# Four layers on a graph: the second batch's attention changes from whole fp32 weights to fp16 high and low parts

## The chip, the cores and the metric

The kernel runs on one core of a Trainium2 chip. The metric is the device time of one execution in microseconds (us). Times inside an execution are counted from the first instruction of the profiled span.

## The reference, cut to what matters

There are 8 batches of 1024 nodes with 128 features (`x`), one dense 1024x1024 matrix `adj`, and four layers, each followed by a residual and a layer norm. Layer 1 is the attention that this change is about:

```python
Q = x @ q
K = x @ k
A = jnp.einsum('bnd,bmd->bnm', Q, K)
A = A / jnp.sqrt(jnp.float32(input_dimension))
A = jnp.tanh(A / 8.0) * 8.0
A = jnp.exp(A) * A_shape            # A_shape is adj
A = A / jnp.sum(A, axis=-1, keepdims=True)
out = A @ x @ v
...
x = _layernorm(x + _L0_gnn_ref(x, adj, ...))   # rows scaled to unit norm
x = _layernorm(x + _L1_gnn_ref(x, adj, ...))   # the attention
x = _layernorm(x + _L2_gnn_ref(x, adj, ...))
x = _layernorm(x + _L3_gnn_ref(x, adj, ...))
```

## The kernel before

All engines run one program each, written out in a fixed order, and meet only at semaphores. The names: PE is the matmul engine, DVE the vector engine, ACT the scalar engine, POOL computes the inverse roots of the norms, SP issues the transfers. Batches are numbered 0 to 7; "the second attention" is that of batch 1.

**Precision by parts.** Most matmuls take an fp32 value as two fp16 tensors, a high part (written by ACT as a copy) and a low part (written by DVE as value minus high part). A product is then three fp16 matmuls: high by high, high by low, low by high.

**One attention** has eight steps t = 0 to 7, one for each block of 128 keys:

- `scores(i, t)` on PE: 6 matmuls of 512 columns into one of two PSUM regions (`r0`, `r1`).
- `exponent(i, t)` on ACT: a Tanh (L414) and an Exp (L416) into slot t % 4 of the fp32 ring `att`.
- `mask(i, t)` on DVE (L907): `att` times `adjT`; it raises the semaphore `pm`.
- For attentions with i >= FULL, `p_hi_part` on ACT (L292, `ph`) and `p_lo_part` on DVE (L912, `pl`) split the slot into the fp16 rings `p_hi` and `p_lo`.
- `attend(i, t)` on PE adds the step to the sums in PSUM `av`. With i < FULL it waits for `pm` and issues 8 fp32 matmuls of 129 columns, with `att` as the stationary and `v_full` as the moving side (L1473). With i >= FULL it waits for `pl` and issues 24 fp16 matmuls (L1482, L1484, L1485) from `p_hi`, `p_lo` and the parts of V (`vhi`, `vlo`, `vhs`).

FULL is 2 before: batches 0 and 1 use whole fp32 weights, batches 2 to 7 use parts. The whole V of batch 1 is written into the memory of `p_lo`, which is free until batch 2; that is why the trace names the fp32 operand of the second attention `p_lo`. A slot of `att` may be overwritten once `attend` has read it (whole weights), or once `p_lo_part` has read it (parts).

**Around the second attention** (PE's `start()`, L1533 on): PE starts with `scores(1, 0)`, finishes `attend(0, 6)` and `attend(0, 7)`, and then alternates `scores(1, t)`, `attend(1, t)` and `adj_x2_part(0, k)` (6 matmuls of 512 columns each, the third layer's product of batch 0). After `adj_x2_part(0, 3)` comes `sum_x2` (L1398), which DVE waits for in `sums_read` (L795). After `adj_x2_part(0, 7)` comes `back(1)`: two parts of `adj_x0`, and then `project` with `w2s` (L1314), which waits for DVE's `y2_lo(0, 1)` (L788), which in turn waits for ACT's `y2_hi(0, 1)`, a copy of what `adj_x2_part(0, 4)` to `(0, 7)` summed.
DVE's own order in this stretch is: masks, and between them the end of batch 0's attention (`row_sums`, residual), its layer norm (`ln_begin` L584 on, root on POOL, `ln_shift` L618, `ln_norm`), `x2_lo`, `sj_step`, `weights_split`, and after the last mask `sums_read`, `sums`, `y2_lo(0, 0)`, `sj_step`, `x0_lo(2)`, `l2_read`, `l2_rank_one`, `y2_lo(0, 1)`. ACT's `copy_x2` writes the high part that `x2_lo` needs.

Of the kernel before, what the change touches and what calls it, by code (L numbers as in the profile page):

```python
# [40 lines left out]
L2_LINKS = 4  # L41
V_CHUNKS = 5
AVW = 130
FULL = 2
RING = 4
AHEAD = 3

# [30 lines left out]
def adj_resnorm(nc, x, adj, adj_t, w_first, w2, w3, rows, out):  # L78
    ctx = ExitStack()
    with ctx:  # L80
# [62 lines left out]
        minus_half = sb("minus_half", [P, C])  # L143
        small = sb("small", [P, 5, 8, C])
        rsum, rinv = sb("rsum", [P, 9]), sb("rinv", [P, C])
        v_full = [t[:].rearrange("p r n -> p (r n)").bitcast(F32)[:, 0:C * AVW].rearrange("p (c d) -> p c d", c=C) for t in (p_hi, p_lo)]
        junk = att[:].rearrange("p r n -> p (r n)").bitcast(F16)
        last_junk = u[:].rearrange("p c d -> p (c d)").bitcast(F16)[:, 0:N]
        row_bufs = [t[:].rearrange("p c d -> p (c d)") for t in (pq, u, tmp)]
# [140 lines left out]
        def _(act):  # L290
# [54 lines left out]
            def copy_x2(b):  # L345
                act.wait_ge(S["ln1_v"], b + 1)
                act.wait_ge(S["ln1_a"], b + 1)
                if not is_first(b, 0):
                    act.wait_ge(S["y2_mm"], 2 * b)
                copy(x2s[:, 0], xas[b % 2][:], X_UP).then_inc(S["x2_hi"], 1)  # L350
# [46 lines left out]
            def v_whole(b, src):  # L397
                for h in range(2):
                    act.wait_ge(S["v_mm"], 2 * b + h + 1)
                    copy(v_full[b][:, half_chunks(h), 0:D], cd(src[:])[:, half_chunks(h)], W_DOWN / LO_UP).then_inc(S["v_hi"], 1)  # L400
# [5 lines left out]
            def exponent(i, t):  # L406
                t8, s = i * C, t % RING
                act.wait_ge(S["s_mm"], t8 + t + 1)
                if RING <= t8 + t < FULL * C + RING:
                    act.wait_ge(S["av_mm"], t8 + t - RING + 1)  # L410
                elif t8 + t >= RING:
                    act.wait_ge(S["pl"], t8 + t - RING + 1 - FULL * C)
                dst = (r1, r0)[(t + (i == 0)) % 2]
                nc.scalar.activation(att[:, s], dst[:], ACT.Tanh, scale=c_tanh).then_inc(S["th"], 1)  # L414
                act.wait_ge(S["th"], t8 + t + 1)
                nc.scalar.activation(att[:, s], att[:, s], ACT.Exp, scale=TANH_CAP).then_inc(S["ex"], 1)  # L416
# [14 lines left out]
            def start():  # L431

                scale_adj(0, 3)
                y0_hi(0, 0, r1[:, half(0)])
                y0_hi(0, 1, r1[:, half(1)])
                degrees(0, 3)
                x0_hi(1)
                for h in range(2):
                    act.wait_ge(S["dg_mm"], h + 1)
                    copy(d_hi[:, half(h)], r0[:, half(h)], 1.0 / ADJ_UP).then_inc(S["dg_hi"], 1)  # L440
                scale_adj(3, C)
                degrees(3, 6)
                act.wait_ge(S["p0_mm"], 2)
                y0_hi(1, 0, m7[:])
                norm(0, 0, xas[0], V_CHUNKS)
                x1t_hi(0, r1)
                degrees(6, 7)
                g_hi(0, r2)
                y0_hi(1, 1, av[:, 2])
                v_whole(0, r1)  # L450
                for t in range(C):
                    exponent(0, t)
                    if t == 5:
                        degrees(7, 8)
                    if t == 6:
                        norm(0, 1, xas[1], V_CHUNKS)
                x1t_hi(1, r0)
                g_hi(1, r1)
                v_whole(1, r0)
                for t in range(C):  # L460
                    exponent(1, t)
                    if t == 3:
                        norm(1, 0, xas[0], V_CHUNKS)
                        copy_x2(0)
                act.wait_ge(S["p0_mm"], 4)
                y2_hi(0, 0)
                x0_hi(2)
# [106 lines left out]
        def _(dve):  # L574
# [304 lines left out]
            def sj_low():  # L879
                return tt(one_sj[:, :, 2], sj[:], one_sj[:, :, 1], ALU.subtract)  # L880
# [96 lines left out]
            def start():  # L977
# [54 lines left out]
                        ln_norm(0, 1, xas[1])  # L1032
                x1t_lo(1, r0)
                g_lo(1, r1)
                row_scales()
                x0_max(2)
                mask(1, 0)
# [2 lines left out]
                    l_ = attention_residual(0, j)  # L1040
                l_.then_inc(S["e1a"], 1)
                mask(1, 1)
                dve.wait_ge(S["e1a"], 1)
                ln_begin(1, 0, xas[0])
                mask(1, 2)
                x0_scale_read(2)
                x0_scales(2)
                ln_shift(1, 0)
                ln_norm(1, 0, xas[0])
                mask(1, 3)  # L1050
                x2_lo(0)
                mask(1, 4)
                sj_ch = Count(dve, S["sj_c"], 0, 5)
                for k_ in range(2):
                    sj_step(sj_ch, 0, k_)
                mask(1, 5)
                weights_split(3, 4)
                w_ch.end()
                mask(1, 6)
                sj_low().then_inc(S["sj_l"], 1)  # L1060
                mask(1, 7)
                l2_ch = Count(dve, S["l2_c"], 0, L2_LINKS)
                sums_read(0, r0)
                sums(0)
                y2_lo(0, 0)
                sj_step(sj_ch, 0, 2, False)
                sj_step(sj_ch, 0, 3)
# [223 lines left out]
        def _(pe):  # L1291
# [197 lines left out]
            def start():  # L1489
# [38 lines left out]
                scores(1, 0)  # L1528
                attend(0, 6)
                attend(0, 7)  # L1530
                pe.wait_ge(S["v_hi"], 4)
                scores(1, 1)
                next_scores(1, 2)  # L1533
                next_scores(1, 3)
# [229 lines left out]
```

## Time and profile before

| what | value |
|---|---|
| median of 3 runs | 659.71 us (659.68 to 660.11) |
| the profiled execution, its own time | 661.49 us |
| its span, first to last instruction | 659.0 us |
| PE busy | 631.6 us, 96% |
| DVE busy | 568.4 us, 86% |
| ACT busy | 400.5 us, 61% |
| mean granted clock of PE | 0.995 |

The profiled execution took 661.49 us, of which 2.49 us lie outside the span. Busy time of PE counts matmuls from their start to a modelled end, and they overlap, so the start-to-start times of its groups are the better measure of what a group costs. Idle time that a view puts in brackets is the time in which an engine stood waiting, with the instruction that ended it.

### The profile page before, as it was taken

What the parts mean: (1) busy time and instruction counts of PE and PEld (TensorE: products, weight loads), DVE (VectorE), ACT (ScalarE), POOL (GpSimd) and SP (SyncE); (2) the same over time, 40 slices, a digit from 0 to 9 for tenths busy, and PEclk for the clock granted to TensorE, in tenths of its full rate; (3) what the DMA queues carried; (4) which work ended last, traced back from release to release, by engine and by line L of the source; (5) the groups of instructions that cost most, each with busy time, mean ns of one, the idle gap of its engine ahead of it and who ended that gap; (6) DMA issues with size and microseconds to landing.
All of it is one profiled execution on the core that took longest, in us unless ns stands there. A gap on an engine that the chain in (4) does not pass through costs nothing.

```text
span 659.0 us, 17533 instructions
## 1 busy us (share of the span) xinstructions
PE 631.6 (96%) x7446; PEld 489.0 (74%) x7446; DVE 568.4 (86%) x1514; ACT 400.5 (61%) x706; POOL 73.4 (11%) x50
## 2 busy tenths in 40 slices
PE   8899899999999999999999999999999999889994
PEld 3457667698677976799667986789667986549894
DVE  6889687889899899889899899889898898989635
ACT  5879583354955669265873659365892649432522
POOL 0101210010002200210002200031002100020002
PEclk9999999999999999999999999999999999999998
DMA  8710000000000200002000200002000000000012
GB/s 334 260 65 1 1 1 1 0 31 6 2 1 2 66 1 2 1 2 66 2 1 1 66 2 1 2 3 66 1 1 2 8 29 1 1 1 2 2 34 65
DMA packets 12589, 18.74 MB, mean 28 GB/s; under 512 B 608, under 2 KB 9056, under 8 KB 12512
## 3 DMA queue, kind: packets, MB, share of 16 engines
q1 hardware_dynamic: 12512, 17.63, 8.1%
q8 instruction: 58, 0.95, 0.6%
q14 instruction: 19, 0.16, 0.1%
HBM read 13.44 MB, written 4.19 MB: 27 GB/s over the span
## 4 chain that ended last, share of the span: by engine, by line
PE 60%; DVE 22%; ACT 10%; issue 4%; POOL 2%; DMA 1%; SPq 0%; ACTq 0%; DVEq 0%; POOLq 0%
PE r L1314 13%; PE r L1316 13%; PE r L1315 13%; ACT att L414 5%; DVE p_lo L912 4%; DVE att L907 4%; PE r L1362 4%; DVE stats L584 2%; POOL small L249 2%; ACT p_hi L292 2%; DVE x L816 2%; PE av L1473 2%; PE r L1320 2%; PE av L1314 2%; PE av L1316 2%
## 5 line engine op out<-in xcount | busy, mean ns | idle before, releaser
L249 POOL TENSOR_TENSOR small<-small,minus_half 128x8 f32<-128x8 f32 (+1 forms) x40 | 69.0, 1729 | 573.7 <-DVE small L611 309.9
L907 DVE TENSOR_TENSOR att<-att,adjT 128x1024 f32<-128x1024 f32 x64 | 78.1, 1222 | 11.9 <-ACT att L416 11.8
L414 ACT ACTIVATE att<-r,coef 128x1024 f32<-128x1024 f32 x64 | 70.5, 1101 | 20.3 <-PE r L1316 19.7
L1314 PE MATMUL r<-xq,a_hi 128*128 128x128 f16 x448 | 76.0, 219 | 0.0
L1315 PE MATMUL r<-xq,a_hi 128*128 128x128 f16 x448 | 76.0, 219 | 0.0
L1316 PE MATMUL r<-xq,a_lo 128*128 128x128 f16 x448 | 76.0, 219 | 0.0
L1314 PE MATMUL r<-rs,a_hi 128*128 128x128 f16 x448 | 75.9, 219 | 0.0
L1315 PE MATMUL r<-rs,a_hi 128*128 128x128 f16 x448 | 75.8, 219 | 0.0
L1316 PE MATMUL r<-rs,a_lo 128*128 128x128 f16 x448 | 75.8, 219 | 0.0
L416 ACT ACTIVATE att<-att 128x1024 f32<-128x1024 f32 x64 | 67.7, 1057 | 2.0
L912 DVE SCALAR_TENSOR_TENSOR p_lo<-p_hi,att 128x1024 f16<-128x1024 f16 x48 | 58.6, 1222 | 0.0
L292 ACT ACTIVATE yT<-r 128x512 f16<-128x512 f32 x18 | 10.6, 595 | 69.6 <-PE r L1316 69.4
L292 ACT ACTIVATE p_hi<-att 128x1024 f16<-128x1024 f32 x48 | 50.1, 1043 | 2.4 <-DVE att L907 2.4
L1315 PEld LDWEIGHTS r<-xq,a_hi 128*128 128x128 f16 x448 | 43.8, 98 | 0.1
L1314 PEld LDWEIGHTS r<-rs,a_hi 128*128 128x128 f16 x448 | 43.8, 98 | 0.0
L1315 PEld LDWEIGHTS r<-rs,a_hi 128*128 128x128 f16 x448 | 43.8, 98 | 0.0
L1314 PEld LDWEIGHTS r<-xq,a_hi 128*128 128x128 f16 x448 | 43.8, 98 | 0.0
L1316 PEld LDWEIGHTS r<-xq,a_lo 128*128 128x128 f16 x448 | 43.8, 98 | 0.0
L1316 PEld LDWEIGHTS r<-rs,a_lo 128*128 128x128 f16 x448 | 43.8, 98 | 0.0
L340 ACT ACTIVATE outb<-outb,small 128x128 f32<-128x128 f32 x56 | 22.8, 481 | 24.2 <-DVE small L618 24.2
L1482 PE MATMUL av<-vhib,p_hi 128*128 128x129 f16 x192 | 33.6, 220 | 3.0 <-DVE p_lo L912 2.9
L1314 PE MATMUL m<-a_hi,x2s 128*128 128x512 f16 x96 | 36.4, 379 | 0.0
(424 smaller groups left out, 2114.9 us busy)
## 6 DMA issues: line engine op xcount, KB each, us to landing
adjT<-in_adj_t SPq DMA_DIRECT2D x8, 512.0 KB, 8.5
out<-outb SPq DMA_DIRECT2D x7, 512.0 KB, 3.4
x<-in_x SPq DMA_DIRECT2D x6, 512.0 KB, 4.8
pq<-in_adj SPq DMA_DIRECT2D x2, 512.0 KB, 8.8
u<-in_adj SPq DMA_DIRECT2D x2, 512.0 KB, 9.3
tmp<-in_adj SPq DMA_DIRECT2D x2, 512.0 KB, 9.8
x2s<-in_adj SPq DMA_DIRECT2D x2, 512.0 KB, 9.6
x<-in_x SPq DMA_DIRECT2D x2, 256.0 KB, 2.7
```

Source lines behind the costliest of these rows:

```text
L249: return nc.gpsimd.tensor_tensor(dst, src, minus_half[:, 0:src.shape[-1]], ALU.pow)
L292: return nc.scalar.activation(dst, src, ACT.Copy, scale=scale, **more)
L340: l_ = nc.scalar.activation(t[:, j], t[:, j], ACT.Identity, scale=small[:, k_, ROOT, j:j + 1], bias=small[:, k_, SHIFT, j:j + 1])
L414: nc.scalar.activation(att[:, s], dst[:], ACT.Tanh, scale=c_tanh).then_inc(S["th"], 1)
L416: nc.scalar.activation(att[:, s], att[:, s], ACT.Exp, scale=TANH_CAP).then_inc(S["ex"], 1)
L907: tt(att[:, s], att[:, s], adjT[:, t, :], ALU.mult).then_inc(S["pm"], 1)
L912: stt(p_lo[:, s], p_hi[:, s], -LO_UP, att[:, s], ALU.mult, ALU.add).then_inc(S["pl"], 1)
L1314: mm(dst, s_hi, m_hi, start=start, stop=False, skip_group_check=True)
L1315: mm(dst, s_hi, m_lo, start=False, stop=False, skip_group_check=True)
L1316: return mm(dst, s_lo, m_hi, start=False, stop=stop, skip_group_check=True)
L1362: l_ = mm(dst[:, a:e], x0s[:, x_part, m], src, start=(n_ == 0 and x_part == 0 and hi is a_hi and a == base), stop=False, skip_group_check= ...
L1482: mm(acc, p_hi[:, s, chunk(j)], vhi[:, t, 0:D + 1], start=(t == 0 and j % 3 == 0), stop=False, skip_group_check=True)
```

## The change

FULL goes from 2 to 1. Batch 0 keeps whole fp32 weights; batch 1 now takes parts, as batches 2 to 7 do. On ACT, V of batch 1 is written as a high part (`v_hi`) in place of whole (`v_whole`), a scaled copy of it (`v_scaled`, 128x1024) is added, and eight `p_hi_part` stand each after the next step's `exponent`. On DVE, `v_lo` (two instructions of 128x512) and eight `p_lo_part` are added. On PE each of eight `attend` steps has 24 fp16 matmuls in place of 8 fp32 ones and waits for `pl` in place of `pm`, and `scores(1, 1)` waits for `v_lo`, since it overwrites the PSUM region that holds V. One small memset of V's constant column at the very start goes. No other instruction changes its place in the order.

```diff
--- before.py
+++ after.py
@@ -41,7 +41,7 @@
 L2_LINKS = 4
 V_CHUNKS = 5
 AVW = 130
-FULL = 2
+FULL = 1
 RING = 4
 AHEAD = 3
 
@@ -143,7 +143,7 @@
         minus_half = sb("minus_half", [P, C])
         small = sb("small", [P, 5, 8, C])
         rsum, rinv = sb("rsum", [P, 9]), sb("rinv", [P, C])
-        v_full = [t[:].rearrange("p r n -> p (r n)").bitcast(F32)[:, 0:C * AVW].rearrange("p (c d) -> p c d", c=C) for t in (p_hi, p_lo)]
+        v_full = [t[:].rearrange("p r n -> p (r n)").bitcast(F32)[:, 0:C * AVW].rearrange("p (c d) -> p c d", c=C) for t in (p_hi,)]
         junk = att[:].rearrange("p r n -> p (r n)").bitcast(F16)
         last_junk = u[:].rearrange("p c d -> p (c d)").bitcast(F16)[:, 0:N]
         row_bufs = [t[:].rearrange("p c d -> p (c d)") for t in (pq, u, tmp)]
@@ -456,12 +456,17 @@
                         norm(0, 1, xas[1], V_CHUNKS)
                 x1t_hi(1, r0)
                 g_hi(1, r1)
-                v_whole(1, r0)
+                v_hi(1, r0)
                 for t in range(C):
                     exponent(1, t)
+                    if t == 0:
+                        v_scaled(1)
+                    if t >= 1:
+                        p_hi_part(1, t - 1)
                     if t == 3:
                         norm(1, 0, xas[0], V_CHUNKS)
                         copy_x2(0)
+                p_hi_part(1, C - 1)
                 act.wait_ge(S["p0_mm"], 4)
                 y2_hi(0, 0)
                 x0_hi(2)
@@ -1032,6 +1037,7 @@
                         ln_norm(0, 1, xas[1])
                 x1t_lo(1, r0)
                 g_lo(1, r1)
+                v_lo(1, r0)
                 row_scales()
                 x0_max(2)
                 mask(1, 0)
@@ -1040,28 +1046,36 @@
                     l_ = attention_residual(0, j)
                 l_.then_inc(S["e1a"], 1)
                 mask(1, 1)
+                p_lo_part(1, 0)
                 dve.wait_ge(S["e1a"], 1)
                 ln_begin(1, 0, xas[0])
                 mask(1, 2)
+                p_lo_part(1, 1)
                 x0_scale_read(2)
                 x0_scales(2)
                 ln_shift(1, 0)
                 ln_norm(1, 0, xas[0])
                 mask(1, 3)
+                p_lo_part(1, 2)
                 x2_lo(0)
                 mask(1, 4)
+                p_lo_part(1, 3)
                 sj_ch = Count(dve, S["sj_c"], 0, 5)
                 for k_ in range(2):
                     sj_step(sj_ch, 0, k_)
                 mask(1, 5)
+                p_lo_part(1, 4)
                 weights_split(3, 4)
                 w_ch.end()
                 mask(1, 6)
+                p_lo_part(1, 5)
                 sj_low().then_inc(S["sj_l"], 1)
                 mask(1, 7)
+                p_lo_part(1, 6)
                 l2_ch = Count(dve, S["l2_c"], 0, L2_LINKS)
                 sums_read(0, r0)
                 sums(0)
+                p_lo_part(1, 7)
                 y2_lo(0, 0)
                 sj_step(sj_ch, 0, 2, False)
                 sj_step(sj_ch, 0, 3)
@@ -1528,7 +1542,7 @@
                 scores(1, 0)
                 attend(0, 6)
                 attend(0, 7)
-                pe.wait_ge(S["v_hi"], 4)
+                pe.wait_ge(S["v_lo"], 2)
                 scores(1, 1)
                 next_scores(1, 2)
                 next_scores(1, 3)
```

The functions that it newly calls for batch 1, as they stand for the later batches:

```python
def v_scaled(b):
    act.wait_ge(S["v_hi"], 2 * (b + 1))
    copy(vhss[b % 2][:, :, 0:D], vhis[b % 2][:, :, 0:D], 1.0 / LO_UP).then_inc(S["v_s"], 1)
def v_lo(b, src):
    for h in range(2):
        hc = half_chunks(h)
        split_lo(vlos[b % 2][:, hc], cd(src[:])[:, hc], W_DOWN, vhis[b % 2][:, hc, 0:D], "v", 2 * b + h + 1)
def p_lo_part(i, t):
    t8, s = i * C, t % RING
    dve.wait_ge(S["ph"], t8 + t + 1 - FULL * C)
    stt(p_lo[:, s], p_hi[:, s], -LO_UP, att[:, s], ALU.mult, ALU.add).then_inc(S["pl"], 1)
```

The next rows are from the order of instructions on DVE, from `mask(1, 1)` to the instruction behind `mask(1, 2)`. In the changed kernel all these lines stand 5 further down, so the mask is L912 and `p_lo_part` is L917. Before:

```order
L907 TENSOR_TENSOR att<-att,adjT 128x1024
L584 BN_STATS stats<-xa 128x6 x8
L599 TENSOR_TENSOR small<-stats 128x8
L600 SCALAR_TENSOR_TENSOR small<-stats 128x8
L601 SCALAR_TENSOR_TENSOR small<-stats 128x8
L608 SCALAR_TENSOR_TENSOR small<-small 128x8
L613 SCALAR_TENSOR_TENSOR small<-small 128x8
L907 TENSOR_TENSOR att<-att,adjT 128x1024
L662 TENSOR_SCALAR xpow<-m 128x1
```

The same place on DVE of the changed kernel:

```order
L912 TENSOR_TENSOR att<-att,adjT 128x1024
L917 SCALAR_TENSOR_TENSOR p_lo<-p_hi,att 128x1024
L589 BN_STATS stats<-xa 128x6 x8
L604 TENSOR_TENSOR small<-stats 128x8
L605 SCALAR_TENSOR_TENSOR small<-stats 128x8
L606 SCALAR_TENSOR_TENSOR small<-stats 128x8
L613 SCALAR_TENSOR_TENSOR small<-small 128x8
L618 SCALAR_TENSOR_TENSOR small<-small 128x8
L912 TENSOR_TENSOR att<-att,adjT 128x1024
L917 SCALAR_TENSOR_TENSOR p_lo<-p_hi,att 128x1024
L667 TENSOR_SCALAR xpow<-m 128x1
```

A `p_lo_part` now stands between each mask and the work that followed it, here ahead of the layer norm of batch 0.

The end of the same stretch on DVE before, from `mask(1, 6)` on: `sj_low`, `mask(1, 7)`, `sums_read` and `sums` (L795 to L805), then `y2_lo(0, 0)`.

```order
L907 TENSOR_TENSOR att<-att,adjT 128x1024
L880 TENSOR_TENSOR one_sj<-sj,one_sj 128x8
L907 TENSOR_TENSOR att<-att,adjT 128x1024
L795 COPY xs<-r 128x3
L802 TENSOR_SCALAR xb<-xs 128x128
L803 TENSOR_TENSOR xs<-xs 128x1
L805 TENSOR_SCALAR xb<-xs,wjp 128x128
L788 SCALAR_TENSOR_TENSOR yT<-m,yT 128x512
```

The same place on DVE of the changed kernel:

```order
L912 TENSOR_TENSOR att<-att,adjT 128x1024
L917 SCALAR_TENSOR_TENSOR p_lo<-p_hi,att 128x1024
L885 TENSOR_TENSOR one_sj<-sj,one_sj 128x8
L912 TENSOR_TENSOR att<-att,adjT 128x1024
L917 SCALAR_TENSOR_TENSOR p_lo<-p_hi,att 128x1024
L800 COPY xs<-r 128x3
L807 TENSOR_SCALAR xb<-xs 128x128
L808 TENSOR_TENSOR xs<-xs 128x1
L810 TENSOR_SCALAR xb<-xs,wjp 128x128
L917 SCALAR_TENSOR_TENSOR p_lo<-p_hi,att 128x1024
L793 SCALAR_TENSOR_TENSOR yT<-m,yT 128x512
```

Three more `p_lo_part` stand here; the last one is behind `sums` and ahead of `y2_lo(0, 0)`.

On ACT before, from the Tanh of `exponent(1, 3)` to the Exp of `exponent(1, 5)`, with the norm and `copy_x2` of batch 0 between:

```order
L414 ACTIVATE att<-r,coef 128x1024
L416 ACTIVATE att<-att 128x1024
L340 ACTIVATE xa<-xa,small 128x128 x3
L292 ACTIVATE x2s<-xa 128x1024
L414 ACTIVATE att<-r,coef 128x1024
L416 ACTIVATE att<-att 128x1024
L414 ACTIVATE att<-r,coef 128x1024
L416 ACTIVATE att<-att 128x1024
```

The same place on ACT of the changed kernel:

```order
L414 ACTIVATE att<-r,coef 128x1024
L416 ACTIVATE att<-att 128x1024
L292 ACTIVATE p_hi<-att 128x1024
L340 ACTIVATE xa<-xa,small 128x128 x3
L292 ACTIVATE x2s<-xa 128x1024
L414 ACTIVATE att<-r,coef 128x1024
L416 ACTIVATE att<-att 128x1024
L292 ACTIVATE p_hi<-att 128x1024
L414 ACTIVATE att<-r,coef 128x1024
L416 ACTIVATE att<-att 128x1024
```

One copy to `p_hi` stands behind each Exp, and it needs the mask of the step before.

## Rows read from the trace of the kernel before

**Rows 1.** The page: busy time by engine; the chain that ended last, by engine.

```profile
PE 631.6 (96%) x7446; PEld 489.0 (74%) x7446; DVE 568.4 (86%) x1514; ACT 400.5 (61%) x706; POOL 73.4 (11%) x50
...
PE 60%; DVE 22%; ACT 10%; issue 4%; POOL 2%; DMA 1%; SPq 0%; ACTq 0%; DVEq 0%; POOLq 0%
```

**Rows 2.** Busy time per engine in two stretches: second attention, third attention.

```profile
85.61:117.96 32.35, 31.06 (x223) 22.94 (x222) 25.50 (x59) 16.15 (x18) 2.55 (x1) 1.00 0.00 1
163.44:193.00 29.56, 29.51 (x269) 18.48 (x269) 26.34 (x40) 26.35 (x27) 0.00 (x0) 1.00 0.01 2
```

**Rows 3.** Tiles av, p_hi and p_lo by shape: duration min/median/max in ns, first and last start.

```profile
L1482 PE MATMUL av<-vhi,p_hi x192: 219/220/231, 170.9 to 498.6; 128*128 128x129 f16 x192
...
L1485 PE MATMUL av<-vhs,p_lo x192: 218/220/220, 171.0 to 498.7; 128*128 128x129 f16 x192
...
L1473 PE MATMUL av<-p_lo,att x128: 273/275/357, 85.7 to 116.6; 128*128 128x129 f32 x128
...
L292 ACT ACTIVATE p_hi<-att x48: 1037/1041/1059, 167.8 to 567.2; 128x1024 f16<-128x1024 f32 x48
...
L292 ACT ACTIVATE p_lo<-r x2: 599/599/599, 76.0 to 76.7; 128x512 f32<-128x512 f32 x2
...
L912 DVE SCALAR_TENSOR_TENSOR p_lo<-p_hi,att x48: 1216/1221/1230, 169.4 to 568.3; 128x1024 f16<-128x1024 f16 x48
```

**Rows 4.** Timeline of PE around second attention, and one third-attention step: start, length.

```profile
85.75 2.03 PE L1473 MATMUL av<-p_lo,att 128*128 128x129 f32 x16
87.62 0.38 PE L1314 MATMUL r<-gb_,x1Tb 128*128 128x512 f16 x1
...
88.91 1.95 PE L1473 MATMUL av<-p_lo,att 128*128 128x129 f32 x16
90.70 0.38 PE L1314 MATMUL r<-gb_,x1Tb 128*128 128x512 f16 x1
...
108.36 0.17 PE L1398 MATMUL r<-one_sj,x2s 128*128 128x3 f16 x1
...
119.54 0.23 PE L1314 MATMUL r<-w2s,yT 128*128 128x128 f16 x1
...
170.90 0.22 PE L1482 MATMUL av<-vhi,p_hi 128*128 128x129 f16 x1
...
172.26 0.38 PE L1314 MATMUL r<-g,x1T 128*128 128x512 f16 x1
```

**Rows 5.** Timeline of DVE; a bracket is idle time before, and its releaser.

```profile
80.50 1.23 DVE L907 TENSOR_TENSOR att<-att,adjT 128x1024 f32<-128x1024 f32 x1 [2.27 <-ACT att L416]
...
85.37 1.23 DVE L907 TENSOR_TENSOR att<-att,adjT 128x1024 f32<-128x1024 f32 x1 [0.76 <-ACT att L416]
86.51 1.64 DVE L584 BATCH_NORM_STATS2 stats<-xa 128x6 f32<-128x128 f32 x8
...
91.50 0.17 DVE L618 SCALAR_TENSOR_TENSOR small<-small 128x8 f32<-128x8 f32 x1 [0.82 <-POOL small L249]
...
96.29 1.23 DVE L907 TENSOR_TENSOR att<-att,adjT 128x1024 f32<-128x1024 f32 x1 [0.86 <-ACT att L416]
...
104.13 1.22 DVE L907 TENSOR_TENSOR att<-att,adjT 128x1024 f32<-128x1024 f32 x1
108.94 0.16 DVE L795 COPY xs<-r 128x3 f32<-128x3 f32 x1 [3.59 <-PE r L1399]
...
118.79 0.69 DVE L788 SCALAR_TENSOR_TENSOR yT<-r,yT 128x512 f16<-128x512 f32 x1 [1.84 <-ACT yT L292]
```

**Rows 6.** Timeline of ACT, second attention; and the root on POOL in the chain.

```profile
84.28 1.06 ACT L416 ACTIVATE att<-att 128x1024 f32<-128x1024 f32 x1
...
101.11 1.11 ACT L414 ACTIVATE att<-r,coef 128x1024 f32<-128x1024 f32 x1 [0.66 <-PE r L1316]
...
88.92 2.56 POOL small L249
```

**Rows 7.** Busy time and granted clock (the 1.00 and 0.77) in two thin stretches.

```profile
65.00:70.00 5.00, 3.20 (x24) 2.40 (x21) 3.40 (x13) 2.10 (x5) 4.20 (x2) 1.00 0.00 2
650.00:655.00 5.00, 0.44 (x8) 0.26 (x5) 4.75 (x27) 0.93 (x3) 2.02 (x2) 0.77 0.36 105
```


## The prediction

> **What bounds the kernel now.** I read the page first: PE is busy for 96% of the span, DVE for 86%, ACT for 61%, and the chain that ended last runs 60% on PE and 22% on DVE [rows 1]. So any microsecond that PE stands still in the middle is likely to reach the end, and DVE is the engine that is close enough to make it stand still. The change touches one stage, so I read that stage alone. In the 32.35 us from the first `attend` of batch 1 to the end of its last product, PE is busy 31.06, DVE 25.50 and ACT 16.15 us [rows 2]: PE sets the pace, DVE has 6.85 us of idle time, ACT 16.2. The third attention, which already uses parts, shows what the form needs: PE 29.51 of 29.56 us with DVE at 26.34 and ACT at 26.35 [rows 2]. There PE never starves, but that stage carries less other DVE work between its masks than this one.
>
> **What the change gives on PE.** A fp32 step starts at 88.91 and what follows it starts at 90.70: 1.79 us for 8 matmuls. A step with parts starts at 170.90 and its follower at 172.26: 1.36 us for 24 [rows 4]. The single durations (275 ns for fp32, 220 ns for fp16 [rows 3]) overlap, so only starts count. The change saves 0.43 us per step, 8 x 0.43 = 3.4 us in all, if PE never waits.
>
> At this place a rule of the Trainium skill speaks against the change. The rows give 1.36 / 24 = 57 ns per pair of weight load and matmul [rows 4]. The page "TensorE: Matmul & The Clock Gate", section "Back-to-back issue gap", puts the sustained pace of such pairs at about 81 ns with 128 columns. By it a step would be an estimated 24 x 81 ns = 1.94 us, longer than the fp32 step, and PE would lose 1.2 us over the eight instead of gaining 3.4. The sum goes by the rows; the other pace is a rival below.
>
> **What it costs on ACT.** Eight copies to `p_hi` at 1.04 us each [rows 3] are 8.3 us, and `v_scaled` is a copy of the same 128x1024 size, about 1.0 us. Writing V's high part instead of whole V is two copies of the same shape at 0.6 us [rows 3], no change. ACT has 16.2 us idle in the stage [rows 2]; its Tanh and Exp move 1 us later per step but stay ahead of the masks that wait behind DVE's own work. Price: nothing. If that cover were gone, ACT would still have only 9.3 us to place in 16.2.
>
> **What it costs on DVE.** `v_lo` is two instructions of 128x512, like the two of `g_lo`, under 1.3 us for both (half of a `p_lo_part` each [rows 3], with their fixed part). They stand in the 2.27 us in which DVE waits before the mask at 80.50 [rows 5], so they cost nothing, and PE's new wait for them (about 78.5) is over when it comes to `scores(1, 1)` behind two fp32 steps (after 81). Eight `p_lo_part` last 1.221 us each [rows 3], as a mask does. Two instructions of this size start 1.14 us apart (85.37 and 86.51 [rows 5]), so they add 8 x 1.14 = 9.12 us. That is more than the 6.85 us that DVE has free [rows 2]. Where it comes out is found by walking through DVE's order; each row is a starting time before, and behind it I put the shift. The price of the order change is in this walk.
>
> 1. `mask(1, 1)` stays at 85.37. `p_hi_part(1, 0)` follows the Exp at 84.28 [rows 6], so it ends about 86.4, and the first `p_lo_part` starts at 86.5 and ends at 87.7. PE's first `attend` started at 85.75 [rows 4], and now starts at about 87.8: a first hole of 2 us, while the layer norm of batch 0 begins at 86.51 + 1.14.
> 2. Ahead of `ln_shift` at 91.50 DVE stood 0.82 us for POOL's root (2.56 us from 88.92 [rows 6]). Two `p_lo_part` stand before it now. DVE is free at 90.68 + 2.28 = 92.96, the root is there at 91.50 + 1.14 = 92.64. Shift: +1.46.
> 3. `mask(1, 4)` at 96.29 had waited 0.86 us for its Exp [rows 5]. That Exp stands behind `copy_x2`, so it shifts by 1.46 to 97.75; DVE is free at 95.43 + 1.46 + 1.14 = 98.03. Shift: +1.74.
> 4. `mask(1, 7)` at 104.13 has three more ahead of it: +1.74 + 3.42 = +5.16, it starts at 109.29. The sixth `p_lo_part`, for t = 5, ended just before, at about 109.30. After the mask and the seventh DVE is free at 109.29 + 2.28 = 111.57.
> 5. `sums_read` at 108.94 waited 3.59 us for `sum_x2` [rows 5]. PE's `attend(1, 5)` now waits for that sixth `p_lo_part`: 109.35, plus 1.36, plus 1.29 for `adj_x2_part(0, 3)` (six matmuls of 512 columns, as 87.62 to 88.91 [rows 4]), plus 0.58 from the start of `sum_x2` to DVE (108.36 to 108.94 [rows 4, 5]): 112.58. Shift: +3.64, and DVE still waits 1.0 us here.
> 6. The eighth `p_lo_part` follows: +4.78. `y2_lo(0, 1)` at 118.79 had 1.84 us idle ahead [rows 5]: DVE reaches it at 116.95 + 4.78 = 121.73, +2.94. PE's side would allow +3.64 - 2 x 0.43 = +2.78. The later one counts: **+2.9 us**.
>
> As a balance: 9.12 added, less 0.82, 0.86 and 1.84 us of holes filled and 2.6 of the 3.59, gives 3.0. PE's `project` at 119.54 [rows 4] moves by this, to 122.5, and the 3.4 us saved on PE lie inside its new holes (2 us each ahead of `attend` 0, 1 and 2, less later).
>
> **What is late next.** In the third attention PE is busy 29.51 of 29.56 us [rows 2] at the same clock, so there is no hole to give the delay back, and `back(1)` is in order behind `project` on all engines. Each transfer of a later batch is released by these same engines. The shift reaches the end whole. Batches 2 to 7 are unchanged.
>
> **The sum.** The profiled execution took 661.49 us (span 659.0); with +2.9 it would take 664.4. It lies 1.78 us above the median of the runs, 659.71; the same shift on the median gives **662.6 us**, slower by 0.44%. Own bounds: at 1.22 us a piece (the full duration, no overlap of starts) the eight cost 0.6 us more, +3.5. If the wait in step 5 did not come about (`attend(1, 5)` had its weights a little earlier), up to 1.0 us goes, +1.9. So this case spans 661.5 to 663.3.
>
> **The rivals.**
> - *DVE hides its new work and PE's saving counts (faster).* PE ahead by up to 3.4 us: 656.3. For it speaks ACT's and DVE's idle time in the stage and the full PE of the third attention [rows 2]. Against it: 9.12 us don't fit into 6.85. It decides at a `p_lo_part` of about 0.8 us or less, (9.12 - 2.9) / 8; the rows show 1.22 in every form [rows 3]. Chance 0.06.
> - *The delay is given back (no change).* Should 2 of the 2.9 us be absorbed in `back(1)`, the time is 660.6. Chance 0.09.
> - *Parts run at a slower pace on PE than in the third attention.* Bounded by the fp32 step, 1.79 us from start to start [rows 4]: step 5 gives +3.64 + 0.43 = +4.07 and the last two steps give nothing back, so PE decides: +4.1 us, 663.8. Against it: 192 fp16 instructions of each form with a median of 220 ns [rows 3], and the 57 ns pace. Chance 0.06. The page named above would make such a step longer still, an estimated +4.5 us in all by the same steps; the trace does not agree with it.
> - *PE's clock falls in the new holes.* Three holes of 2 us each between 85.6 and 97 leave PE about half busy. Granted clock stayed at 1.00, 2.4 GHz, where it was busy 3.20 of 5 us, and fell (0.77 in the mean) only where it was busy 0.44 of 5 [rows 7]. At 1.2 GHz the next 6.6 us of matmuls take twice as long; part of that hides in the waits for DVE, so up to +6.6 on top, 666 to 669. Chance 0.05.
>
> **How the numbers follow.** My case has a chance of 0.74. A measurement of this kernel can tell about 0.2%, 1.3 us, from no change: 658.4 to 661.0. Slower: 0.74 + 0.06 + 0.05 = 0.85; same 0.09; faster 0.06. The range leaves out the faster case, the absorbed one and the fallen clock (0.20) and reaches from my lower bound to the slow pace, 661.5 to 663.8, with 0.3 to 0.4 us more on both sides, since each of the walk's three places where a bracket is subtracted from a start is good to about 0.1 us: 661.2 to 664.2.
>
> **What the profile after would show.** Right: PE's first `attend` of batch 1 at about 87.8; brackets of about 2 us on PE that end with `p_lo` L917, three of them; DVE without a bracket before `ln_shift` and `mask(1, 4)`, with about 1 us before `sums_read`; `project` at 122.4; every later row of PE later by the same 2.9. Wrong: DVE brackets as long as before (then ACT is the cause, and the copies were not free), `project` at 119 or earlier, or steps of `attend` that start more than 1.4 us ahead of their followers.

## The result, and the profile after

The change made the kernel slower: the ratio to the kernel before is 1.004, with a 95% interval from 1.0026 to 1.0053. It is a ratio of means over 12 executions each, 663.31 against 660.80 us, a difference of 2.5 us. The medians are 663.57 and 660.26 us, 3.3 us apart. The forecast was +2.9 us, 662.6 us, in a range from 661.2 to 664.2; it started from a median of 659.71 us over three executions, and on 660.26 us the same +2.9 gives 663.2 us. A few executions of several kernels, the kernel before among them, took over 100 us longer than the rest (773.6, 937.56 and 1677.14 us), and no ratio in this document counts them.

A part of each time lies outside the profiled span. In the changed kernel this is 2.0 to 2.2 us; in the kernel before it was 2.49 us in the profiled execution and 2.4 us in the mean of the 62 that were measured beside the experiments. Why it differs is not known. It makes a difference of times about 0.3 us smaller than what happens inside the span.

The page of the changed kernel, busy time by engine and the chain that ended last:

```profile
PE 628.9 (95%) x7510; PEld 484.7 (73%) x7510; DVE 578.4 (87%) x1523; ACT 409.0 (62%) x715; POOL 73.4 (11%) x50
...
PE 60%; DVE 24%; ACT 8%; issue 4%; POOL 2%; DMA 1%; SPq 0%; ACTq 0%; DVEq 0%; POOLq 0%
```

Against [rows 1], PE has 2.7 us less to do and DVE 10.0 us more; DVE's share of the chain rose from 22 to 24%. The span grew from 659.0 to 661.4 us.

Busy time per engine (PE, PEld, DVE, ACT, POOL), granted clock, DMA: the thin part of the second attention, the whole of it, and the third attention of the changed kernel:

```profile
85.61:97.00 11.39, 6.14 (x70) 4.16 (x69) 11.18 (x31) 10.44 (x13) 2.55 (x1) 1.00 0.00 0
85.61:121.00 35.39, 28.73 (x293) 18.98 (x292) 33.88 (x67) 24.23 (x27) 2.55 (x1) 1.00 0.00 1
...
166.00:195.60 29.60, 29.55 (x272) 18.56 (x270) 26.21 (x40) 26.51 (x27) 0.00 (x0) 1.00 0.01 1
```

In [rows 2] PE was the full engine of this stage and DVE had 6.85 us free. Now DVE is busy 33.88 of 35.39 us and PE only 28.73. In the first 11.39 us PE works barely more than half the time, and its granted clock is still 1.00. The third attention is as it was.

Timeline of PE of the changed kernel, from the first `scores` of batch 1 to `project`; a bracket is the hole ahead, with what ended it:

```profile
76.63 0.39 PE L1328 MATMUL r<-gb_,x1Tb 128*128 128x512 f16 x1
...
87.75 0.22 PE L1496 MATMUL av<-vhib,p_hi 128*128 128x129 f16 x1 [1.99 <-DVE p_lo L917]
...
89.10 0.38 PE L1328 MATMUL r<-gb_,x1Tb 128*128 128x512 f16 x1
...
92.18 0.23 PE L1496 MATMUL av<-vhib,p_hi 128*128 128x129 f16 x1 [1.62 <-DVE p_lo L917]
...
96.63 0.23 PE L1496 MATMUL av<-vhib,p_hi 128*128 128x129 f16 x1 [1.63 <-DVE p_lo L917]
...
104.90 0.23 PE L1496 MATMUL av<-vhib,p_hi 128*128 128x129 f16 x1 [0.20 <-DVE p_lo L917]
...
108.93 0.23 PE L1496 MATMUL av<-vhib,p_hi 128*128 128x129 f16 x1 [1.21 <-DVE p_lo L917]
...
121.97 0.23 PE L1328 MATMUL r<-w2s,yT 128*128 128x128 f16 x1
```

A step with parts is as short as forecast: 87.75 to 89.10 is 1.35 us against 1.79 [rows 4]. Five of the eight steps wait for a low part. A bracket counts from the modelled end of the matmul before, so start to start the holes are longer: `scores` from 89.10 would be done at 90.39 (1.29 us), and the next step starts at 92.18, a hole of 1.79 us where the bracket says 1.62. In this way the five are 7.5 us. The steps save 8 x 0.44 = 3.5 us, and a hole of 1.5 us for a Tanh is gone. Before, this line of PE's timeline had it (1.45 us from start to start):

```profile
95.23 0.39 PE L1314 MATMUL r<-gb_,x1Tb 128*128 128x512 f16 x1 [1.29 <-ACT att L414]
```

So the delay is 7.5 - 3.5 - 1.5 = 2.5 us.

Timeline of DVE of the changed kernel, at the places of [rows 5]:

```profile
80.37 1.23 DVE L912 TENSOR_TENSOR att<-att,adjT 128x1024 f32<-128x1024 f32 x1 [0.93 <-ACT att L416]
...
86.38 1.22 DVE L917 SCALAR_TENSOR_TENSOR p_lo<-p_hi,att 128x1024 f16<-128x1024 f16 x1
87.52 1.64 DVE L589 BATCH_NORM_STATS2 stats<-xa 128x6 f32<-128x128 f32 x8
...
92.74 0.16 DVE L623 SCALAR_TENSOR_TENSOR small<-small 128x8 f32<-128x8 f32 x1
...
97.63 1.22 DVE L912 TENSOR_TENSOR att<-att,adjT 128x1024 f32<-128x1024 f32 x1
...
108.86 1.22 DVE L912 TENSOR_TENSOR att<-att,adjT 128x1024 f32<-128x1024 f32 x1
...
112.17 0.16 DVE L800 COPY xs<-r 128x3 f32<-128x3 f32 x1 [0.95 <-PE r L1413]
...
121.23 0.68 DVE L793 SCALAR_TENSOR_TENSOR yT<-r,yT 128x512 f16<-128x512 f32 x1
```

The hole before the first mask shrank from 2.27 to 0.93 us and took `v_lo` in. The holes of 0.82, 0.86 and 1.84 us are gone, and that of 3.59 us is 0.95.

The start of the kernel, with its loads, takes a little longer or shorter from one execution to the next: `scores(1, 0)` starts between 74.90 and 77.90 us in the profiled executions of the kernels below. So from here on a place in the program is counted from the start of the first matmul of `scores(1, 0)`. The three columns of places are from one profiled execution of each kernel (us, and the difference to the kernel before); the ratio is of the mean times of all its executions. In the row "no low part" the places are from a second measurement of the same kernel.

| kernel | `sums_read` (DVE) | `project` (PE) | transposes of x3 (PE) | time, ratio and 95% interval |
|---|---|---|---|---|
| before | 32.18 | 42.78 | 52.92 | |
| changed | 35.54 (+3.36) | 45.34 (+2.56) | 55.47 (+2.55) | 1.004 (1.0026 to 1.0053) |
| no low part | 31.38 (-0.80) | 41.17 (-1.61) | 51.31 (-1.61) | 0.9965 (0.995 to 0.9979) |
| DVE filler | 35.22 (+3.04) | 45.82 (+3.04) | 55.96 (+3.04) | 1.0047 (1.0029 to 1.0064) |
| ACT filler | 32.68 (+0.50) | 43.27 (+0.49) | 53.41 (+0.49) | 1.0007 (0.9994 to 1.0021) |
| parts from t = 4 | 32.94 (+0.76) | 42.74 (-0.04) | 52.88 (-0.04) | 1.0002 (0.9989 to 1.0015) |
| parts from t = 5 | 31.82 (-0.36) | 41.62 (-1.16) | 51.76 (-1.16) | 0.9981 (0.9966 to 0.9997) |
| parts from t = 6 | 32.19 (+0.01) | 41.99 (-0.79) | 52.13 (-0.79) | 0.9992 (0.9981 to 1.0003) |
| split and rank-one later | 34.15 (+1.97) | 43.93 (+1.15) | 55.78 (+2.86) | 1.0065 (1.0043 to 1.0088) |
| split later | 34.15 (+1.97) | 45.71 (+2.93) | 55.84 (+2.92) | 1.0039 (1.0025 to 1.0054) |
| four masks on POOL | 40.58 (+8.40) | 50.37 (+7.59) | 60.50 (+7.58) | 1.0096 (1.0078 to 1.0114) |

Behind the transposes of x3 nothing moves any more in the changed kernel: the first `scores` of batch 2 stand at 85.39 us before and 87.94 in the changed kernel, and from there to the end of the span it is 496.85 and 496.83 us. The whole change of time is made between the first `attend` of batch 1 and `project`.

### The profile page after: what moved, and what is told of

Same layout as the page of the kernel before. It is cut to its first block, busy times and chain, and to the rows that moved or that the text cites. A ratio compares the mean times of both kernels' runs of the same rounds, so it can differ in the third digit from the quotient of the medians.

```text
span 661.4 us, 17680 instructions
## 1 busy us (share of the span) xinstructions
PE 628.9 (95%) x7510; PEld 484.7 (73%) x7510; DVE 578.4 (87%) x1523; ACT 409.0 (62%) x715; POOL 73.4 (11%) x50
## 4 chain that ended last, share of the span: by engine, by line
PE 60%; DVE 24%; ACT 8%; issue 4%; POOL 2%; DMA 1%; SPq 0%; ACTq 0%; DVEq 0%; POOLq 0%
PE r L1328 13%; PE r L1330 13%; PE r L1329 13%; DVE p_lo L917 5%; DVE att L912 5%; PE r L1376 4%; ACT att L414 4%; DVE stats L589 2%; DVE x L821 2%; PE r L1334 2%; POOL small L249 2%; PE av L1496 2%; ACT p_hi L292 2%; PE av L1328 2%; PE av L1499 2%
## 5 line engine op out<-in xcount | busy, mean ns | idle before, releaser
L912 DVE TENSOR_TENSOR att<-att,adjT 128x1024 f32<-128x1024 f32 x64 | 78.0, 1221 | 9.7 <-ACT att L416 9.6
L917 DVE SCALAR_TENSOR_TENSOR p_lo<-p_hi,att 128x1024 f16<-128x1024 f16 x56 | 68.2, 1220 | 0.0
L292 ACT ACTIVATE p_hi<-att 128x1024 f16<-128x1024 f32 x56 | 58.4, 1043 | 4.8 <-DVE att L912 4.8
L1496 PE MATMUL av<-vhib,p_hi 128*128 128x129 f16 x256 | 44.9, 220 | 9.6 <-DVE p_lo L917 9.5
L1499 PE MATMUL av<-vhsb,p_lo 128*128 128x129 f16 x256 | 44.8, 220 | 0.0
L1498 PE MATMUL av<-vlob,p_hi 128*128 128x128 f16 x256 | 44.8, 219 | 0.0
```

The lines of the kernel that those rows point to most:

```text
L292: return nc.scalar.activation(dst, src, ACT.Copy, scale=scale, **more)
L912: tt(att[:, s], att[:, s], adjT[:, t, :], ALU.mult).then_inc(S["pm"], 1)
L917: stt(p_lo[:, s], p_hi[:, s], -LO_UP, att[:, s], ALU.mult, ALU.add).then_inc(S["pl"], 1)
L1496: mm(acc, p_hi[:, s, chunk(j)], vhi[:, t, 0:D + 1], start=(t == 0 and j % 3 == 0), stop=False, skip_group_check=True)
L1498: mm(acc[:, 0:D], p_hi[:, s, chunk(j)], vlo[:, t, :], start=False, stop=False, skip_group_check=True)
L1499: l_ = mm(acc, p_lo[:, s, chunk(j)], vhs[:, t, 0:D + 1], start=False, stop=(t == C - 1), skip_group_check=True)
```

## The experiments

Theory A is that of the prediction: DVE's eight passes for the low part set the delay, and the shorter steps on PE are a real gain that they hide. Theory B: ACT's eight copies, or the step with 24 matmuls itself, set it.

**No low part.** The changed kernel, with `attend` of batch 1 taking the high part twice:

```diff
 def p_lo_part(i, t):
+    if i == 1:
+        return
     dve.wait_ge(S["ph"], t8 + t + 1 - FULL * C)
...
-                pe.wait_ge(S["pl"], (i - FULL) * C + t + 1)
+                low = p_hi if i == 1 else p_lo
+                if i == 1:
+                    pe.wait_ge(S["ph"], t + 1)
+                else:
+                    pe.wait_ge(S["pl"], (i - 2) * C + t + 1)
...
-                    l_ = mm(acc, p_lo[:, s, chunk(j)], vhs[:, t, 0:D + 1], ...)
+                    l_ = mm(acc, low[:, s, chunk(j)], vhs[:, t, 0:D + 1], ...)
```

> The changed kernel without the eight p_lo_part of batch 1: DVE loses its eight new passes, and the third of the three products of each step takes the high part p_hi in place of p_lo, so that PE has the same 24 matmuls; attend waits for the high part. (The low-part product of batch 1 is therefore another number.) Theory A, DVE's passes set the delay and the shorter PE steps are a real gain that they hide: PE's saving of 8 x 0.43 us comes out in part, limited by ACT's copies and the mask order; first attend 0.6 us later than before, project 1.4 us earlier than before, time 0.2% under the kernel before. Theory B, ACT's eight copies or the 24-matmul form itself set the delay: the time stays 0.3 to 0.5% above the kernel before.

Not shown: the Tanh of batch 1 no longer waits for a low part before it overwrites a slot of `att`. The ratio is 0.9965, 2.3 us under the kernel before. The same kernel once more, for its profile:

> The kernel without the low-part passes once more, for its profile: project 1.4 us earlier than before when counted from the first scores of batch 1 (42.78 us before), so about 41.4 us; PE without a bracket ahead of attend that ends with p_lo.

Timeline of PE in that execution; every bracket between `scores(1, 1)` and `project`:

```profile
85.56 0.22 PE L1502 MATMUL av<-vhib,p_hi 128*128 128x129 f16 x1 [0.54 <-ACT p_hi L292]
...
91.55 0.23 PE L1502 MATMUL av<-vhib,p_hi 128*128 128x129 f16 x1 [0.21 <-ACT p_hi L292]
...
94.86 0.39 PE L1330 MATMUL r<-gb_,x1Tb 128*128 128x512 f16 x1 [1.78 <-ACT att L414]
```

`project` comes at 41.17 us, where 41.4 was expected. With ACT's copies, `v_lo` and the 24-matmul steps all in place, the kernel is faster than before; leaving out DVE's eight passes, and the wait for them, takes 4.2 us off the changed kernel (45.34 to 41.17). Theory B falls: neither ACT's copies nor the form of the step can set the delay. Of the 3.5 us that the shorter steps save, 1.6 come out here, since PE now waits for a high part twice and for one Tanh 0.49 us longer than before (1.78 against 1.29 us).

**DVE's passes alone.** The kernel before, with a pass of the same shape and types at each of the eight places:

```diff
+spare = sb("spare", [P, 4, N], F16)
...
+            def filler(t):
+                stt(spare[:, t % 4], a_hi[:, t], -LO_UP, adjT[:, t, :], ALU.mult, ALU.add)
...
                 mask(1, 1)
+                filler(0)
...
                 mask(1, 2)
+                filler(1)
```

> The kernel before, with whole fp32 weights for batch 1, plus eight DVE passes of the same shape and types as p_lo_part at the same eight places of DVE's order; they write a spare tile that nobody reads. ACT and PE are untouched. Theory A: DVE's passes alone give most of the delay. PE's steps wait for masks, not for a low part, so it comes out about 1 us smaller: project +2.0 us, time +0.3%. Theory B (ACT or PE's form is the cause): within 0.1% of the kernel before.

1.0047: as slow as the changed kernel, with PE and ACT untouched. `project` moved by +3.04 us, 1.0 more than expected. Timeline of PE of this kernel:

```profile
95.96 0.39 PE L1326 MATMUL r<-gb_,x1Tb 128*128 128x512 f16 x1 [2.64 <-ACT att L415]
96.19 0.53 PE L1327 MATMUL r<-gb_,x1Tb 128*128 128x512 f16 x1
96.51 0.63 PE L1328 MATMUL r<-gb_,x1Tb 128*128 128x512 f16 x1
...
98.22 0.63 PE L1326 MATMUL m<-a_hi,x2s 128*128 128x512 f16 x1
...
100.25 0.50 PE L1485 MATMUL av<-p_lo,att 128*128 128x129 f32 x3
```

And its busy time and granted clock in stretches of 2 us:

```profile
94.00:96.00 2.00, 0.04 (x1) 0.04 (x2) 2.00 (x3) 1.97 (x3) 0.00 (x0) 1.00 0.00 0
96.00:98.00 2.00, 2.00 (x6) 0.77 (x7) 2.00 (x3) 2.00 (x2) 0.00 (x0) 0.57 0.00 0
98.00:100.00 2.00, 2.00 (x6) 0.71 (x5) 2.00 (x3) 1.97 (x2) 0.00 (x0) 0.58 0.03 8
100.00:102.00 2.00, 2.00 (x18) 1.94 (x17) 1.93 (x4) 1.14 (x2) 0.00 (x0) 1.00 0.00 0
```

After a hole of 2.64 us the granted clock fell, to 1.2 GHz for nearly all of the next 4 us. The twelve matmuls from 95.96 to 100.25 take 4.29 us instead of 2 x 1.29, so 1.7 us are lost to the clock. On PE the +3.04 us are this loss and 1.35 us more of waiting for the Tanh, which stands behind a layer norm that DVE's passes put off. The delay by passes alone was thus not seen by itself. An estimate from DVE's timeline of this kernel: it stood 0.64 us ahead of `sums_read` and 0.70 us ahead of `y2_lo(0, 1)`, both times waiting for the slowed PE; without the fall it could have been 1.3 us earlier, and `project` at about +1.7 us, where +2.0 was expected.

**ACT's copies alone.** The kernel before, with ACT's added work and its waits:

```diff
+            def filler(t):
+                act.wait_ge(S["pm"], C + t + 1)
+                act.wait_ge(S["av_mm"], C)
+                copy(p_hi[:, t % RING], att[:, t % RING], 1.0 / LO_UP)
...
                     exponent(1, t)
+                    if t == 0:
+                        copy(vhss[1][:, :, 0:D], cd(a_hi[:, 0]), 1.0 / LO_UP)
+                    if t >= 1:
+                        filler(t - 1)
```

> The kernel before plus ACT's part of the change alone: eight copies of att to p_hi at the same places, each waiting for its mask, and one copy of 128x1024 where v_scaled stands; nobody reads them. Theory A: the copies cost little, because ACT has 16 us idle; they make the last masks later where ACT has to wait for a mask before it goes on to the next Tanh: project +0.3 to +0.7 us, time +0.05 to +0.1%. Theory B (ACT): +2 us or more, time +0.3% or more.

1.0007, interval on both sides of 1, and +0.49 us at `project`. The prediction priced ACT at nothing; alone it costs half a microsecond. The waits for masks are not the reason, since no copy up to there has a bracket. Ahead of the norm of batch 0 ACT had one hole of 2.19 us, and three copies of 0.95 us each, from start to start, now stand before it. The norm on ACT before, in the kernel with ACT's copies, and in the changed kernel:

```profile
91.70 1.26 ACT L340 ACTIVATE xa<-xa,small 128x128 f32<-128x128 f32 x3 [2.19 <-DVE small L618]
...
93.41 1.25 ACT L340 ACTIVATE xa<-xa,small 128x128 f32<-128x128 f32 x3
...
92.93 1.26 ACT L340 ACTIVATE xa<-xa,small 128x128 f32<-128x128 f32 x3 [0.71 <-DVE small L623]
```

Counted from `scores(1, 0)` the norm starts 0.57 us later with the copies, and the Tanh behind it, for which PE waits, 0.49 us later. In the changed kernel the same hole has 0.71 us left, because DVE brings the norm's input still later: there ACT's copies cost nothing.

**Parts for the last three steps only.** Steps 0 to 4 of batch 1 keep whole weights. V of batch 1 is written whole and, for the second half of the keys only, in parts as well (cut to the main lines, against the changed kernel):

```diff
+PART_FROM = 5
+WHOLE = C + PART_FROM
...
+v_full.append(sb("v_all", [P, C, AVW])[:])
...
-                v_hi(1, r0)
+                v_whole(1, r0)
+                copy(vhis[1][:, half_chunks(1), 0:D], cd(r0[:])[:, half_chunks(1)], W_DOWN).then_inc(S["v_x"], 1)
...
-                    if t >= 1:
+                    if t > PART_FROM:
                         p_hi_part(1, t - 1)
...
-                if i < FULL:
+                if i * C + t < WHOLE:
                     pe.wait_ge(S["v_hi"], 2 * (i + 1))
```

> The changed kernel with parts only for the last three steps of batch 1 (t = 5, 6, 7); steps 0 to 4 keep whole fp32 weights, and the whole V of batch 1 lies in a tile of its own (4160 bytes a partition). DVE then has three of the eight new passes, and they stand where it had 3.59 and 1.84 us idle before. Theory A: three steps save 0.43 us each on PE and the three passes cost at most what the holes hold: project 1.0 us earlier than before, time 0.15% under the kernel before. Rival: a step with parts costs PE a wait wherever it stands: time equal to the kernel before or up to 0.2% above.

0.9981, and `project` 1.16 us earlier: this version is 0.2% faster than the kernel before, and 0.6% faster than the changed one by the two ratios. Of the 1.27 us between the mean times, 0.35 lie outside the span; the spans differ by 0.93 us. Timeline of DVE there, `sums_read`:

```profile
108.66 0.16 DVE L805 COPY xs<-r 128x3 f32<-128x3 f32 x1 [0.95 <-PE r L1415]
```

Two of the three passes stand ahead of it and eat 2.3 us of the hole of 3.59. PE has no bracket ahead of any of the three steps with parts.

**One step more, one step less.** The same with `PART_FROM = 4` and `PART_FROM = 6`:

> The late-parts kernel with one step more in parts: t = 4 to 7, four of the eight passes on DVE. Theory A, by the walk: the fourth pass stands between mask 4 and the row sums of the third layer, where DVE has no hole left, so it is paid in full while PE gains 0.43 us: project +0.1 us against the kernel before, that is 1.1 to 1.3 us later than with three; time 0.0% (-0.1 to +0.1%). Rival (each step in parts is worth the same wherever it stands): 0.1% faster than with three steps, 0.25% under the kernel before.

> The late-parts kernel with only two steps in parts, t = 6 and 7. Theory A: both passes lie in DVE's holes (3.59 and 1.84 us before), so PE's 2 x 0.43 us come out less what V's extra parts cost: project 0.7 us earlier than before, time 0.1% under the kernel before, that is 0.4 us slower than three steps (1.16 us earlier in its trace) and 0.7 us faster than four (0.04 us). Rival (the gain of the three-step kernel is chance): project at the same 42.8 us from the first scores of batch 1 as before.

`project` stood at -0.04 and -0.79 us, where +0.1 and -0.7 were expected. The fourth pass costs 1.12 us at `project`, about what one pass takes in DVE's order (1.14 us): there it is paid in full, and PE, which has a shorter step, stands 1.21 us for a low part instead. The intervals of the times of neighbours overlap, so the order 6, 5, 4 rests on the profiled executions; that of 5 against 4 also on 0.9981 and 1.0002, whose intervals overlap by little.

**Pieces of DVE's order moved.** The changed kernel, nothing added or taken away:

```diff
-                weights_split(3, 4)
-                w_ch.end()
                 mask(1, 6)
...
                 sums(0)
                 p_lo_part(1, 7)
+                weights_split(3, 4)
+                w_ch.end()
...
-                l2_rank_one(l2_ch, z_all, 0)
                 y2_lo(0, 1)
+                l2_rank_one(l2_ch, z_all, 0)
```

> The changed kernel with two pieces of DVE's order moved, nothing added or taken away: weights_split(3, 4), 1.76 us, goes from between masks 5 and 6 to behind the last p_lo_part, and l2_rank_one goes behind y2_lo(0, 1). Theory A: the delay is made of the passes that stand ahead of what PE waits for, not of their sum. Ahead of sum_x2 there are then 1.76 us less: sums_read 1.4 us earlier than in the changed kernel, project 1.0 to 1.5 us earlier; time 0.15 to 0.2% under the changed kernel, 0.2 to 0.25% above the kernel before. Rival (DVE's total decides): as the changed kernel, +0.4%.

The walk was right up to `project` (1.4 us earlier than in the changed kernel) and my conclusion from it was wrong: the time is 1.0065. The two pieces were only put off. The transposes of x3, which need what `l2_rank_one` starts, stand at 55.78 us, 0.3 us later than in the changed kernel, and the gain is gone. These +2.86 us over the kernel before are 0.43%; the rest of the 0.65% was not in the profiled execution. Most of it comes from two of the six, 665.99 and 667.42 us against 663.72 to 664.40, and what they met is not known. With the first move alone:

> The changed kernel with weights_split(3, 4) moved behind the last p_lo_part, and l2_rank_one left at its place: one of the two moves of the kernel with both. That one had project 1.4 us earlier than the changed kernel and the transposes of x3 0.3 us later, and was slower in the end. Theory A (DVE is full from the first p_lo_part to y2_lo(0, 1), so a piece moved inside this stretch only changes which wait is short): sums_read 1.4 us earlier than in the changed kernel, but project at the same time or up to 0.5 us later; time +0.4 to +0.5% against the kernel before. Rival (what stands ahead of sum_x2 decides): +0.2%.

`sums_read` comes 1.39 us earlier than in the changed kernel, `project` 0.37 us later, ratio 1.0039. The rival of the earlier run, that DVE's total decides, is what both show. With the piece gone, DVE comes to `sums_read` earlier but stands 1.33 us there in place of 0.95, and these 0.38 us are the 0.37 by which `project` is later. From the first low part to the norm behind `project`, DVE has no hole that this move could fill; it only makes one longer.

**Masks on POOL.** The changed kernel with four products moved to the idle engine:

```diff
+ON_POOL = (3, 4, 5, 6)
...
+            for t in ON_POOL:
+                pool.wait_ge(S["ex"], C + t + 1)
+                nc.gpsimd.tensor_tensor(att[:, t % RING], att[:, t % RING], adjT[:, t, :], ALU.mult).then_inc(S["pm_p"], 1)
...
-                mask(1, 3)
-                mask(1, 4)
-                mask(1, 5)
-                mask(1, 6)
```

> The changed kernel with four masks of batch 1 (t = 3 to 6) on POOL, which is idle there, in place of DVE. No row of these kernels shows how long POOL takes for a 128x1024 product of two tensors; the walk gives the same for 2.3 and 2.8 us. Theory A: DVE is relieved of 4 x 1.14 us: project 2.1 to 2.6 us earlier than in the changed kernel, time equal to the kernel before (0 to +0.15%). Rival (a POOL product takes 4 us or more, or slows DVE's own instructions beside it): as the changed kernel or slower, +0.4% and above, and DVE's passes longer than 1.22 us in the rows.

1.0096, `project` +7.6 us: the rival, and more. Timeline of POOL, then of DVE, of this kernel:

```profile
91.07 2.34 POOL L271 TENSOR_TENSOR att<-att,adjT 128x1024 f32<-128x1024 f32 x1
98.11 2.36 POOL L271 TENSOR_TENSOR att<-att,adjT 128x1024 f32<-128x1024 f32 x1 [4.69 <-ACT att L420]
101.14 2.63 POOL L271 TENSOR_TENSOR att<-att,adjT 128x1024 f32<-128x1024 f32 x1 [0.68 <-ACT att L420]
104.18 2.88 POOL L271 TENSOR_TENSOR att<-att,adjT 128x1024 f32<-128x1024 f32 x1 [0.41 <-ACT att L420]
```

```profile
91.37 2.07 DVE L630 SCALAR_TENSOR_TENSOR small<-small 128x8 f32<-128x8 f32 x1
...
99.01 2.54 DVE L924 SCALAR_TENSOR_TENSOR p_lo<-p_hi,att 128x1024 f16<-128x1024 f16 x1 [1.81 <-ACT p_hi L296]
101.47 3.38 DVE L899 TENSOR_TENSOR tmp<-xa,bias 128x1024 f32<-128x1024 f32 x1
104.89 1.22 DVE L901 TENSOR_REDUCE sj<-tmp 128x8 f32<-128x1024 f32 x1
106.14 0.96 DVE L902 CAST one_sj<-sj 128x8 f16<-128x8 f32 x1
```

A product on POOL takes 2.3 to 2.9 us. A DVE instruction with two inputs that meets one hardly moves until POOL is done: 2.07 us for one of 8 elements that takes 0.16 in the changed kernel, 2.54 and 3.38 us for passes of 1.22. The first ends at 93.44, when POOL's product ends (93.41). It works the other way too: the two longer products, 2.63 and 2.88 us, started while such a DVE pass was still running (to 101.55 and 104.85). The sum over a row at 104.89, with one input, ran beside a product in its usual 1.22 us. In this kernel the clock fell as well, to 0.50 from 110 to 112 us, behind a hole of 2.56 us on PE, so not all of the +7.6 us is DVE's.

## Why the prediction was right

1. *What the change gives on PE.* Right: 1.35 us per step against 1.79. The Trainium skill's pace of 81 ns a pair ("TensorE: Matmul & The Clock Gate", "Back-to-back issue gap") does not hold here; 24 pairs in 1.35 us are 56 ns.
2. *ACT at nothing.* Right for the changed kernel, but not for the reason given. The 16.2 us that ACT had free in the stage did not decide it, but the 2.19 us ahead of one norm. They are too short for three copies and cost 0.49 us where the copies are the only addition; DVE's longer delay hides that.
3. *`v_lo` in the hole before the mask.* Right: the mask stands at 80.37 with 0.93 us of the hole left, and PE's wait for it is not in the trace.
4. *The walk along DVE.* Forecast against the trace, as shifts: `ln_shift` +1.46, now +1.24 by the clock of the trace, or +1.37 counted from `scores(1, 0)`; `mask(1, 4)` +1.74, now +1.47; `mask(1, 7)` +5.16, now +4.86; `sums_read` +3.64, now +3.36; `y2_lo(0, 1)` +2.94, now +2.57. So the walk is 0.1 to 0.4 us too late, and the term that was mis-sized is the length of the holes. DVE's free time was taken as the start of an instruction less its bracket. But a bracket counts from the end of the instruction before, and DVE's next one starts some 0.09 us ahead of that end where it waits for nothing (86.51 against 85.37 + 1.23 [rows 5]). The walk loses this at `ln_shift`, at `mask(1, 4)` and at `y2_lo(0, 1)`. At `mask(1, 4)` it loses about as much again, mostly because `x2_lo` stood some 0.07 us for ACT's `copy_x2` before, a wait that has no bracket and that a pass now fills.
5. *The new wait ahead of `sums_read`*, 1.0 us: 0.95. It is the part of the delay that the sum of passes and holes doesn't give: PE's `attend(1, 5)`, which waits for the sixth low part, had become later than DVE.
6. *Nothing gives the delay back.* Right to 0.02 us over the last 497.
7. *The rival of the clock* did not come about in the profiled execution of the changed kernel: its longest hole is 1.99 us and the granted clock 1.00 throughout the stage. It was near: in two experiments (DVE filler, masks on POOL) holes of 2.64 and 2.56 us were followed by it, while holes of 2.41 and 2.46 us (masks on POOL, split and rank-one later) were not. Its price, up to 6.6 us, rested on no row: the fall in the DVE filler cost PE 1.7 us.
8. *The size.* The walk's +2.9 us stands against +2.55 us at the same places of the two traces. That the time fits as well is in part luck: the 0.3 to 0.4 us that the walk is too long were not known, nor was the change of 0.3 us outside the span, and the base of three executions was 0.5 us under the later median of twelve.

What stays open: the executions of the changed kernel lie between 661.95 and 664.42 us. The five longest, from 663.84 us, have a mean granted clock of 0.994, and six of the other seven 0.996 or 0.997 (that of 662.08 us has 0.993). Where in the span they lost it isn't known for these. Three profiled executions of other kernels with 0.993 or 0.994 (ACT filler, split and rank-one later, parts from t = 6) had a fall at 9 to 13 us, well ahead of this stage, and their `scores(1, 0)` stands at 77.19 to 77.90 us, later than in all the others. So a fall at the start is the likely reason, but it is not shown.

## What to carry to other kernels

A trade of PE time for DVE time is settled by the holes of DVE in that very stretch of its order, one by one: 9.1 us of passes against 6.9 us of holes lost 2.5 us although PE had 3.4 us less to do, and three such passes alone, put where the holes were, gained 1.2. The sum of free time over the stage misled: ACT had 16.2 us free for 9.3 us of new work, and with that work alone it still came half a microsecond late at the one place where it mattered. Moving work about inside a stretch that has become full only chooses which wait is short; follow it past the next engine's first wait before counting a gain.

## What the runs showed of the hardware

- A DVE instruction with two inputs stands still beside a POOL product of two tensors: 0.16 us became 2.07, 1.22 became 3.38. The page "SBUF — State Buffer" of the Trainium skill, section "Who interferes with whom", describes this as a port pair that one of the two engines holds for a whole instruction. It counts DVE instructions with two inputs and also casts among those that can take the pair, and reductions not. The rows agree on all three: a conversion of 8 elements with a single input took 0.96 us instead of 0.18, and a reduction beside a product kept its 1.22 us.
- The granted clock of PE stayed at 1.00 with holes of 1.99, 1.62 and 1.63 us in 11.4 us, and fell to 0.57 right after one of 2.64 us. One such fall cost PE 1.7 us, while the change itself cost 2.55.
- 24 fp16 pairs of weight load and matmul take 1.35 us, 8 fp32 pairs 1.79 us, each from start to start: three fp16 products are the cheaper form for PE, if the engines that make the parts have time.
